# Context attention of a decoder: order of DMA transposes, place of the angle computation, and rotary steps split around the probabilities' low part

## The reference, cut to what matters

```
q = rms_norm((x @ Wq.T).reshape(b, 128, 16, 128), q_norm_w)
kv_in = concatenate([context, x], axis=1)                 # 128 + 128 rows
k = rms_norm((kv_in @ Wk.T).reshape(b, 256, 4, 128), k_norm_w)
v = (kv_in @ Wv.T).reshape(b, 256, 4, 128)
q, k = rope(q, positions), rope(k, positions)             # x*cos + rotate_half(x)*sin
probs = softmax(einsum(q, k) / sqrt(128))                 # 4 query heads share a key head
x = layernorm(x + (einsum(probs, v)) @ Wo.T)
```

## Time and profile before

| what | us |
|---|---|
| median of three runs | 3083.76 (3081.76 to 3086.56) |
| the profiled execution | 3087.13 |
| its span, first to last instruction | 3085.3 |
| first maximum of pass 0 | 521.30 |
| first maximum of pass 1 | 579.72 |
| first maximum of pass 14 | 1271.64 |
| one middle pass, first maximum to first maximum | 795.94 to 848.67, 52.7 |

### The profile page before, as it was taken

One profiled execution on the slowest core, in us unless ns is written; L12 is line 12 of the kernel. 1 busy time (PEld: TensorE's weight loads), 2 busy tenths in 40 slices (PEclk: granted clock), 3 DMA queues, 4 the chain that ended last, 5 costly groups with the idle time before them and its releaser, 6 DMA issues. The chain is left out here.

```text
span 3085.3 us, 47741 instructions
## 1 busy us (share of the span) xinstructions
PE 2672.4 (87%) x16117; PEld 1503.0 (49%) x16380; DVE 1938.7 (63%) x3457; ACT 1605.3 (52%) x3757; POOL 1326.5 (43%) x1334
## 2 busy tenths in 40 slices
PE   6788885688888888857996899998989999999998
PEld 4676662344443444423443565665664444444443
DVE  5788986577777777747855788887563233332325
ACT  7999864555555555537434686776532212222111
POOL 4888977756656565603333311111142212222121
PEclk8999997899999999989997899999989999999999
DMA  4111105443334343433003000000012011111101
GB/s 160 41 55 43 45 25 144 99 80 67 77 73 78 71 78 74 76 91 115 1 1 110 22 19 18 14 15 22 15 67 77 31 63 62 61 63 35 62 30 68
DMA packets 287059, 181.05 MB, mean 59 GB/s; under 512 B 243585, under 2 KB 248065, under 8 KB 284706
## 3 DMA queue, kind: packets, MB, share of 16 engines
q1 hardware_dynamic: 286882, 178.74, 22.1%
HBM read 111.25 MB, written 4.52 MB: 38 GB/s over the span
## 5 line engine op out<-in xcount | busy, mean ns | idle before, releaser
L2065 POOL TENSOR_TENSOR s_state<-s_state,s_ct 128x512 f32<-128x512 f32 x256 | 326.3, 1303 | 80.2 <-DVE s_state L2240 78.1
L779 POOL TENSOR_TENSOR m_aTl<-m_prod,m_aTh 128x512 bf16<-128x512 f32 x88 | 101.7, 1155 | 583.9 <-ACT m_aTh L855 583.9
L2240 DVE TENSOR_TENSOR_SCAN s_state<-s_decay,s_psd 128x512 f32<-128x512 f32 x256 | 301.9, 1209 | 66.0 <-PE s_psd L2385 32.8
L1044 DVE TENSOR_TENSOR m_prod<-m_bank,m_gated 128x512 f32<-128x512 f32 x88 | 60.9, 692 | 437.3 <-ACT m_gated L853 437.3
L853 ACT ACTIVATE m_gated<-m_bank 128x512 f32<-128x512 f32 x88 | 52.5, 597 | 435.6 <-PE m_bank L1166 435.6
L1156 PE MATMUL m_bank<-m_xTl,m_wh 128*128 128x512 bf16 x704 | 267.4, 380 | 3.1 <-ACT m_wh L819 1.0
L1155 PE MATMUL m_bank<-m_xTh,m_wh 128*128 128x512 bf16 x671 | 255.0, 380 | 2.4 <-DVE m_prod L1044 2.4
L1572 ACT ACTIVATE a_prob<-a_pss,a_shift,a_qscale 128x256 f32<-128x256 f32 x256 | 141.0, 560 | 172.7 <-DVE a_shift L1686 172.6
L2385 PE MATMUL s_psd<-ident,s_v 128*128 128x128 f32 x1024 | 164.3, 285 | 43.1 <-DVE s_state L2240 22.2
L2141 ACT ACTIVATE s_decay<-s_dt,s_nega 128x508 f32<-128x508 f32 x256 | 181.7, 711 | 19.0 <-DVE s_state L2240 19.0
L1705 DVE SCALAR_TENSOR_TENSOR a_pp<-a_prob,a_rtotal,a_pp 128x256 bf16<-128x256 f32 x256 | 175.3, 745 | 21.7 <-ACT a_pp L1588 21.7
(11 more groups left out here) (509 smaller groups left out, 7924.0 us busy)
## 6 DMA issues: line engine op xcount, KB each, us to landing
s_ct<-ssm_bc SPq DMA_DIRECT2D x64, 256.0 KB, 3.1
m_scale<-moe_scale SPq DMA_DIRECT2D x64, 256.0 KB, 3.1
m_stage<-in_moe_w_dram SPq DMA_DIRECT2D x16, 768.0 KB, 4.8
m_stage<-in_moe_w_dram SPq DMA_DIRECT2D x8, 864.0 KB, 7.8
X<-in_x_dram SPq DMA_DIRECT2D x4, 1024.0 KB, 11.2
a_cf<-in_ctxT_dram SPq DMA_DIRECT2D x16, 256.0 KB, 2.9
a_wstage<-in_xa_wq_dram SPq DMA_DIRECT2D x8, 512.0 KB, 3.7
a_wstage<-in_xa_wo_dram SPq DMA_DIRECT2D x8, 512.0 KB, 4.4
```

The costliest lines, as they stand in the source:

```text
L2065: pool.tensor_tensor(h, h, ct[t % 4][:, s * P:(s + 1) * P].unsqueeze(1).broadcast_to([P, KB, P]), ALU.mult).then_inc(weighted, 1)
L2240: dve.tensor_tensor_scan(state[i % RING][:, :], decay[t % 2][:, s, :, :].rearrange("p m t -> p (m t)"), ps_d[i % 2][:, :], 0.0, ALU.mult, ...
```

## The change

It has three parts, all inside `stage_xattn`.

1. On SP's queue, `turn_probs(s, g)` now stands ahead of `turn_chunks(s + 1, g)`. The weight loads of pass 0 stood behind the chunk transposes and ahead of those of the probabilities; they are now ahead of both.
2. On GpSimd, `angles(s + 2)` moves from round 1 (between `turned_low` of the first and of the second chunk) to round 0, behind `x_copy` and ahead of the layer norm's power and of `front`.
3. On VectorE, `chunk` is cut in two. Part 0 is the sum of squares, the cosine product and the mean plus epsilon; part 1 is the two sine products. For the even chunk of a round, part 0 stays ahead of `prob_low` and part 1 goes behind it; for the odd chunk both stay together. Chunk 6 has part 1 only, so it goes behind `prob_low` whole. Part 0 waits for `roped` of chunk c - 2 (the reader of `mul`), and only part 1 for `t_low` (the reader of `rot`), where before the whole chunk waited for `t_low` at its head.

```diff
--- before.py
+++ after.py
@@ -1395,11 +1395,11 @@
                 for g in range(4):
                     if g == 0 and not last_x:
                         context(s + 2)
-                    if not last:
-                        turn_chunks(s + 1, g, 1 - p)
                     if start == 0 and g:
                         wl.sync(sp, wlow, first_wo + 2 * g + 1, min(first_wo + 2 * g + 3, nchunks))
                     turn_probs(s, g)
+                    if not last:
+                        turn_chunks(s + 1, g, 1 - p)
 
             sp.dma_start(posi[:, :, :].rearrange("p a s -> p (a s)"), positions).then_inc(loaded, 16)
             sp.dma_start(fq[:, :], freqs).then_inc(loaded, 16)
@@ -1493,7 +1493,6 @@
                     if not last_x:
                         if g == 0:
                             x_copy(s + 2)
-                        if g == 1:
                             angles(s + 2)
                         if g == 2:
                             c_low_part(s + 2, p)
@@ -1646,8 +1645,10 @@
                 dve.wait_ge(angle.sem, angle.at(n))
                 dve.tensor_scalar(ang[:, :, :], ang[:, :, :], -PI, PI, ALU.max, ALU.min).then_inc(sines.sem, 1)
 
-            def chunk(n, c, j):
+            def chunk(n, c, j, part):
                 r = c % 2
+                if c >= 6 and part == 0:
+                    return
                 if c >= 6:
                     dve.wait_ge(v_high.sem, v_high.at(n, c - 5))
                     dve.tensor_tensor(vl[j][:, c - 6, :], ps_p[c % 4][:, :], vh[j][:, c - 6, :], ALU.subtract).then_inc(v_low.sem, 1)
@@ -1661,8 +1662,15 @@
                 src = ps_p[c % 4][:, :].rearrange("p (h d) -> p h d", h=4)
                 m = mul[r][:, :].rearrange("p (h d) -> p h d", h=4)
                 o = rot[r][:, :].rearrange("p (h d) -> p h d", h=4)
+                if part == 1:
+                    if c >= 2 or late(n, 1):
+                        dve.wait_ge(t_low.sem, t_low.at(n, c - 1) if c >= 2 else t_low.at(n - 1, 5 + c))
+                    dve.tensor_tensor(o[:, :, 0:64], src[:, :, 64:128], sinw[:, 0, :].unsqueeze(1).broadcast_to([P, 4, 64]), ALU.mult)
+                    dve.tensor_tensor(o[:, :, 64:128], src[:, :, 0:64], sinw[:, 1, :].unsqueeze(1).broadcast_to([P, 4, 64]),
+                                      ALU.mult).then_inc(rope_mul.sem, 1)
+                    return
                 if c >= 2 or late(n, 1):
-                    dve.wait_ge(t_low.sem, t_low.at(n, c - 1) if c >= 2 else t_low.at(n - 1, 5 + c))
+                    dve.wait_ge(roped.sem, roped.at(n, 2 * c - 2) if c >= 2 else roped.at(n - 1, 2 * c + 10))
                 if c or late(n, 1):
                     dve.wait_ge(summed_e.sem, summed_e.at(n, c) if c else summed_e.at(n - 1))
                 dve.tensor_reduce(ss[:, :], sq[:, :].rearrange("p (h d) -> p h d", h=4), AX.X, ALU.add).then_inc(summed.sem, 1)
@@ -1672,9 +1680,6 @@
                     dve.wait_ge(power.sem, power.at(n, c) if c else power.at(n - 1))
                 dve.tensor_scalar(sse[:, :], ss[:, :], 1.0 / HD if c < QC else 1.0, EPS if c < QC else HD * EPS,
                                   ALU.mult, ALU.add).then_inc(summed_e.sem, 1)
-                dve.tensor_tensor(o[:, :, 0:64], src[:, :, 64:128], sinw[:, 0, :].unsqueeze(1).broadcast_to([P, 4, 64]), ALU.mult)
-                dve.tensor_tensor(o[:, :, 64:128], src[:, :, 0:64], sinw[:, 1, :].unsqueeze(1).broadcast_to([P, 4, 64]),
-                                  ALU.mult).then_inc(rope_mul.sem, 1)
 
             def maxima(s, g, p):
                 dve.wait_ge(scored.sem, scored.at(s, g + 1))
@@ -1719,8 +1724,10 @@
                     if g == 0 and not last_x:
                         x_low_part(s + 2, p)
                     if not last:
-                        chunk(s + 1, 2 * g, 1 - p)
+                        chunk(s + 1, 2 * g, 1 - p, 0)
                     prob_low(s, g)
+                    if not last:
+                        chunk(s + 1, 2 * g, 1 - p, 1)
                     if g:
                         attn_low(s, g - 1)
                     elif start != 0:
@@ -1728,7 +1735,8 @@
                     if g == 2 and not last_x:
                         bound(s + 2)
                     if not last:
-                        chunk(s + 1, 2 * g + 1, 1 - p)
+                        for part in range(2):
+                            chunk(s + 1, 2 * g + 1, 1 - p, part)
                     if g == 1 and start is None:
                         ln.vector_end(dve, s - 2)
 
@@ -1747,10 +1755,12 @@
             for g in range(4):
                 if g == 2:
                     bound(1)
-                chunk(0, 2 * g, 0)
+                for part in range(2):
+                    chunk(0, 2 * g, 0, part)
                 if g < 2:
                     wl.vector(dve, wlow, 4 * g + 4, 4 * g + 6)
-                chunk(0, 2 * g + 1, 0)
+                for part in range(2):
+                    chunk(0, 2 * g + 1, 0, part)
                 if g < 2:
                     wl.vector(dve, wlow, 4 * g + 6, 4 * g + 8)
             turns(turn, dve)
```

## The result

The changed kernel takes 3046.69 us (median of 4 runs, 3042.45 to 3048.91) against 3084.49 us (3081.76 to 3086.56) for the kernel before beside it: ratio 0.9876, 95% interval 0.9859 to 0.9893. That is 37.8 us less. The forecast was 18.4 us less and a range that ended at 3054: the sign was right, the size was less than half of it. Of that 36.9 lie in the context attention and 8.9 behind it, where the code is the same (1.0 was lost ahead of it). The part behind it took between 1699 and 1710.5 us in the profiles of all the kernels here, so it is not counted as gain.

What follows compares the result with a forecast made beforehand. No engine is full; a chain of waits through VectorE, ScalarE and GpSimd binds. Stretches sum to -0.8 us a pass (-10.4 over passes 1 to 13), pass 0 gives -8: 3083.8 - 18.4 = 3065.4 us, range 3054 to 3082.

Steps and rivals of the forecast that it cites:

- Round 0 up to the shift of round 1: From a pass's first maximum: low part runs alone, 1.67 us instead of 3.46; gain 0.6 us a pass.
- Shift of round 1 to shift of round 2: Second stretch of a pass: a 0.92 us wait and collisions of 0.79 and 0.74 go; gain 1.9 us.
- rival 1: Round 2's shift loses the race to GpSimd's subtraction and pays 1.15 us: 3080 us; chance 0.14.
- Shift of round 2 to the exponentials of round 3: Third stretch: chunk 2's transpose, now behind the probabilities, makes chunk 4's high part on ScalarE wait; loss 1.0 us.
- Rival 2: Chunk transposes behind the probabilities land after 5.5 us, delaying round 3's high part and exponentials: 3095 us; chance 0.07.
- Exponentials of round 3 to the next pass: Last stretch: chunk 6's low part behind the probabilities' costs 0.6 us, angles may add 0.1; loss 0.7 us.
- Pass 14 nets nothing; pass 15 has no chunks: Last two passes: pass 14 has no angles to gain by, chunk 6 to lose by; no gain counted.
- TensorE pays, but has some 8 us of slack: TensorE pays for SP's late transposes, but VectorE's next maximum did not wait: some 8 us slack a pass.
- Pass 0: Weight loads ahead of the transposes on SP cut ScalarE's 15.8 us of waits; between 0 and 15.8, taken as -8.
- Rival 4: More gain: collisions fall better or chunk 2's transpose is hidden, and pass 0 gives 15.8 us: 3053 us; chance 0.14.
- The weighed rule: GpSimd and VectorE's shared SBUF port pair is an exclusive lock for a whole instruction; power disagrees, shift and low part agree.
- rival 3: Every GpSimd instruction stops a two-input VectorE one: power holds round 0's low part 0.7 us; 3074 us; chance 0.1.

Runs made afterwards that it cites:

- experiment 9: Old and new order swapped in passes 14 and 15 alone: new ones put in the kernel before, 3079.3 us; old ones put in the kernel after, 3048.6 us.
- Experiment 2: Two parts of three: the kernel after with one of SP's order, early angles or split rotary steps undone; without SP's new order, 11.5 us slower.
- q_no_order: The kernel after with SP's order of before (chunk transposes, weight loads, probabilities); angles and split kept: 11.5 us slower than after.
- experiment 8: Chunk 2's transpose alone ahead of the probabilities in round 2, on the kernel after with chunk 6 ahead of the low part: 3033.8 us, 0.9834.
- experiment 4: The kernel after with chunk 6's low part ahead of the low part of the probabilities again: 3038.2 us, 0.9856.
- experiment 6: After with chunk 6 ahead, plus SP's old order: in rounds 2 and 3 (split in round 0 only), 3048.9 us; in round 3 alone, 3063.3 us.
- experiment 3: The kernel before with only pass 0's weight loads moved ahead of the chunk transposes on SP: 3087.8 us, 1.0001.
- experiment 1: Each part alone on the kernel before: SP's order 6 us slower, early angles 3059.5 us, split rotary steps within 4 us of before.

## Why the prediction fell short

The sum by places, in the profiles, forecast and measured: passes 2 to 13, -9.6 and -19.7 us; passes 0 and 1, -8.8 and -10.1; pass 14, 0 and -1.3; pass 15 with the tail, 0 and -5.8 (the medians of experiment 9 give 2 to 4 for these two passes). Together -18.4 and -36.9. Two steps failed: the gain of a middle pass was set too low, mostly in round 0, and the last two passes were set at nothing.

- **Round 0 up to the shift of round 1: the mis-sized term.** Forecast -0.6, measured -1.06 (17.12 to 16.06 us, mean of passes 2 to 13). The low part ran alone, 1.66 us, as said. Of the 1.8 us that this saves I let 1.2 come back by "two collisions and a later GpSimd" (the prediction's words make it all 1.8, which its sum does not); 0.6 came back. I had put the mean of chunk 1 at 13.8 and the next maximum's end at 15.75. In the pass shown the mean ended at 13.5 (794.79 + 0.78) and the maximum at 15.3, the shift at 15.84 instead of 16.4. The collision of an angle instruction with the first shift, priced at 0.2, occurs in every other pass only: in the one shown the shift took 0.16 us, and the low part started at 8.67 instead of 8.95. The other passes end this stretch at 16.27, where before they ended it at 17.22. The mean and the shift of round 1 were held by GpSimd as said, but I had rounded up at each hand-over, 0.28 us in all. So the collisions were rightly foreseen and all priced to the cautious side.
- **Shift of round 1 to shift of round 2: right.** Forecast 12.45, measured 12.35. The shift took 0.16; rival 1 did not occur, by 0.16 us (810.27 against 810.43). Experiment 2 shows that the margin is made by the new order: with the old one the shift takes 0.90, this stretch is 0.75 us longer and the kernel 11.5 us slower (`q_no_order`; of these 5.6 lie in passes 2 to 13).
- **Shift of round 2 to the exponentials of round 3: right, but read too simply.** Forecast 13.8, measured 13.77. ScalarE waited 0.33 us for the transpose behind its sines, where I had said that the clamp's chain ends 0.3 us sooner. From this follows what I did not say: only 0.3 to 0.4 of the loss of 1.0 is the price of SP's order (experiment 8). The rest is that ScalarE waits 3.46 us for the clamp, behind which stand its table load and the high part: VectorE's own order, by the split. Rival 2 fell: the chunk transposes landed in 3.1 to 4.9 us, median 3.3.
- **Exponentials of round 3 to the next pass: right in kind.** Forecast 9.25, measured 9.13; chunk 6's 0.7 is shown by experiment 4.
- The four stretches account for the 0.84 us a pass that was missing. Their means over passes 2 to 13 changed by -1.06, -1.99, +0.83 and +0.58, where -0.6, -1.9, +1.0 and +0.7 were forecast: 0.46 in round 0 and 0.1 to 0.2 in each of the others, all to the cautious side. Over these passes that is 10 of the 18 us by which the forecast fell short, 5.5 of them in round 0.
- **"Pass 14 nets nothing; pass 15 has no chunks": wrong.** In after pass 14 won 0.9 us in round 0 and 0.6 in each of the next two stretches, and lost 0.9 in the last; with the new orders in passes 14 and 15 alone it won nothing (47.5 us), so this gain seems to come from what runs ahead of it. In pass 15 I counted what VectorE issues and not what it waits for: before it waited 2.80 and 0.76 us for TensorE's scores there (0.61 in after), and the tail is TensorE's alone. I gave no reason for setting these two at nothing, and they are another 7 of the missing 18 us in the profiles.
- **"TensorE pays, but has some 8 us of slack": wrong for the next kernel.** Busy time is no measure of slack for an engine that works in order behind one transpose. In before x was transposed 5.7 us into the pass and ScalarE took it at 6.2, a margin of 0.5 us in an engine that is idle for 8. In experiment 6 x came at 7.4, and that costs 1.2 us a pass.
- **Pass 0: too high, and the cause wrong.** Forecast -8 for pass 0 and -0.8 for pass 1, measured -5.38 and -4.75; that the two together come near is luck. I took the -8 from the 15.8 us of the earlier trace rows; experiment 3 removed that wait and won nothing by the medians.
- **Rival 4 had the nearest number (3053) by another way.** None of its conditions came true: the shift of round 1 still ended with GpSimd's sum (797.92 against 797.90), ScalarE still waited for chunk 2's transpose, and pass 0 gave 5.4 us and not 15.8.
- **The weighed rule.** GpSimd's power at 790.92 ran beside the low part, which took its 1.66 us: rival 3 fell. The Trainium skill, "SBUF — State Buffer", section "SBUF: two separate sides", has a GpSimd instruction that reads SBUF lock the shared port pair, for the whole of its time, against a VectorE instruction with two SBUF inputs; these rows differ for the 128x4 power, in each of the 12 middle passes. For the 128x512 subtraction against the shift (0.90 beside it, 0.16 without) the trace agrees.

## What to carry to other kernels

Cost a change by stretches between two hand-overs of the same kind, and then test each part alone and each left out: here the parts were +6, -28 and -1 us alone (medians of experiment 1 less 3087.1) and -38 together, and the part that loses alone is worth 11.5 us in company. Ask of each queue order who waits in the *next* pass too: after a gain elsewhere the cover that hid a late transfer may be gone. Look at the clock before you price a late transfer: the same start, 3.8 us into the pass, cost nothing at the full clock and 1.2 us at the lower one. And don't price several small uncertain collisions all to one side: their sum was here 10 us of the missing 18.

## What the hardware showed unexpectedly

- TensorE's clock can fall behind a wait and makes it dearer. In before, behind each of the 15 idle times of 4.7 to 5.5 us between 560 and 1380 us, products of 128x512 took 0.63 us instead of 0.38 (granted clock 0.51 in the windows of experiments 6 and 9, the lower of its two levels, 1.2 GHz). The idle time alone does not tell: behind 2.1 to 2.5 us there were four times 0.38 and once 0.63 in before, and in after 3.43 us (783.67) left the products at 0.38 and 3.52 us (680.68) at 0.63.
- A 128x4 power of GpSimd (1.18 us) doesn't disturb four two-input VectorE instructions of 128x256 beside it (1.66 us, as alone), while beside GpSimd's sums, products and subtractions of 128x512 the same four take 2.6 to 3.5 us (in the middle passes of before and after).
